# Graph-network kernel on one core: the node half of the gate weight loaded as 32x32 blocks and turned by VectorE

## The chip, the cores and the metric

One Trainium2 chip, one of its cores. The metric is the device time in microseconds of one execution. A core has TensorE (PE, matmul), VectorE (DVE), ScalarE (ACT), GpSimd (POOL) and SyncE (SP), which here only issues transfers; ScalarE can issue transfers too. All engines run their own instruction lists and meet by semaphores. Sixteen DMA engines move data between HBM and SBUF for the core. TensorE contracts over the 128 partitions, so both operands of a product must have the summed index on the partitions; a weight that lies the other way has to be turned first.

## The reference

Eight graphs of eight nodes (64 nodes, 768 features) pass four blocks, each with a residual and a layer norm. The change is in the first block, L0: two rounds of a relational convolution (RGCN) and a gate.

```python
def _gate(h, q, Wg, bg, Wq, bq):
    h3 = h.reshape(B, N, F)
    hg = jnp.einsum('bnf,gf->bng', h3, Wg[:, :F])
    qg = jnp.einsum('blf,gf->blg', q, Wg[:, F:]) + bg
    attn = jax.nn.sigmoid(hg[:, :, None, :] + qg[:, None, :, :])
    qi = jnp.einsum('bnlf,blf->bnf', attn, q)
    alpha = jax.nn.sigmoid(jnp.einsum('bnf,gf->bng', h3, Wq[:, :F]) + jnp.einsum('bnf,gf->bng', qi, Wq[:, F:]) + bq)
    hn = alpha * jnp.tanh(qi) + (1.0 - alpha) * h3
...
h = jax.nn.relu(_rgcn(x, W_rel1, W_root1, b1, src, dst, edge_type))
h = _gate(h, query_embs, Wg, bg, Wq, bq)
h = jax.nn.relu(_rgcn(h, W_rel2, W_root2, b2, src, dst, edge_type))
h = _gate(h, query_embs, Wg, bg, Wq, bq)
```

The gate weight Wg is [768, 1536]. Its left half (the node half) multiplies h, its right half (the query half) the queries. Both are summed over their second index, so both have to be turned. Everything is float32.

## The kernel before

All weights of 768x768 live in seven slots W[0] to W[6] of [128, 6, 768]: row block k of 128 rows is W[s][:, k, :]. The table PLAN says which weight is loaded into which slot and in how many transfers. SyncE issues the weight loads in one written-out order; where a slot is still in use, it waits on a semaphore first, and everything behind it in its list waits too.

TensorE turns a weight in groups: `turn_weight` makes three 128x128 transposes into one PSUM bank (a group), and VectorE or ScalarE copies the bank into the turned weight (`copy_group`). A half of 768x768 takes 12 groups, 36 transposes. Groups are numbered over the whole kernel: the query half of Wg, the queries, the node half (from G_H), and then Wq (from G_QH). The semaphore `turned` counts the groups.

The order of the program up to the first gate is this. TensorE turns the query half and the queries and multiplies them in eight query units (`query_unit`, six chunks each), whose results go to qg. GpSimd meanwhile makes constants and splits the biases into three bfloat16 parts; VectorE builds tables from the edge lists (hot_src in one instruction of 1536 columns, hot_dst in two of 512), from which TensorE counts the edges. Then come the 36 transposes of the node half, which was loaded into slot 3 and goes turned into slot 4 (WgT_h), then the first half of unit 4, the mixing of the nodes (`mix`), the rest of unit 4, and the RGCN: four `project` calls with the three relations and the root weight. Root is loaded into slot 3, so its load waits until the node half is turned. After the RGCN, VectorE takes relu into h, TensorE turns h (with the six EARLY groups of Wq around it) and multiplies it by WgT_h (`project(nodeT, WgT_h, ...)`).

The result hg is split on VectorE into hi, mid and low; ScalarE and GpSimd copy parts of it into `stack`. The first gate then goes over 32 tiles of 128x768. For each tile TensorE spreads rows of the stack (L1395), VectorE adds qg (L913), ScalarE takes the sigmoid (L689), GpSimd (20 tiles, L609) or VectorE (12 tiles, L905) multiplies by the queries, and TensorE sums (L1343). Between the tiles TensorE does the chunks of units 6 and 7 (UNIT_AT) and the other 18 groups of Wq (LATE_AT, from tile 13). Unit 5 (SPLIT_UNIT) stands whole between projection and gate. The second round uses the same turned weights.

At the end of the first gate SyncE loads four small tables into qk (L510, L512), in 768 runs of 16 or 4 bytes each.

## Time and profile before

| | before |
|---|---|
| time, median of 3 runs | 270.37 us (269.51 to 270.51) |
| the profiled execution, its own time | 270.35 us |
| its span (first to last instruction) | 268.5 us |
| granted clock of TensorE | full, in all 40 slices |
| TensorE busy | 251.3 us, 94% |
| VectorE busy | 158.6 us, 59% |
| HBM read | 52.17 MB, 195 GB/s over the span |

Times in the profile are microseconds from the start of the span. TensorE works almost throughout, so its busy share does not tell which of its work matters; the chain of work that ended last does. A busy time of an engine that nobody waits for costs nothing. Instructions that issue transfers are not counted as busy and are shown as SPq or ACTq.

### The profile page before, as it was taken

What the parts mean: (1) busy time and instruction counts of PE and PEld (TensorE: products, weight loads), DVE (VectorE), ACT (ScalarE), POOL (GpSimd) and SP (SyncE); (2) the same over time, 40 slices, a digit from 0 to 9 for tenths busy, and PEclk for the clock granted to TensorE, in tenths of its full rate; (3) what the DMA queues carried; (4) which work ended last, traced back from release to release, by engine and by line L of the source; (5) the groups of instructions that cost most, each with busy time, mean ns of one, the idle gap of its engine ahead of it and who ended that gap; (6) DMA issues with size and microseconds to landing.
All of it is one profiled execution on the core that took longest, in us unless ns stands there. A gap on an engine that the chain in (4) does not pass through costs nothing.

```text
span 268.5 us, 4957 instructions
## 1 busy us (share of the span) xinstructions
PE 251.3 (94%) x2065; PEld 130.9 (49%) x2065; DVE 158.6 (59%) x283; ACT 91.5 (34%) x155; POOL 86.3 (32%) x76
## 2 busy tenths in 40 slices
PE   8899999999999999899999998889998988999994
PEld 4565874454435543356775222224573443435572
DVE  0866450015999999943015999996567267514422
ACT  2323340033657996412001667672302013013000
POOL 7790000003599999700000677870000000000000
PEclk9999999999999999999999999999999999999999
DMA  7999996996002967500699940003999636000001
GB/s 242 373 402 400 402 362 211 379 400 269 2 0 61 410 236 256 102 2 0 163 407 401 402 158 2 0 2 94 363 405 401 264 99 256 0 2 0 2 0 29
DMA packets 21895, 53.46 MB, mean 199 GB/s; under 512 B 4201, under 2 KB 4969, under 8 KB 21874
## 3 DMA queue, kind: packets, MB, share of 16 engines
q1 hardware_dynamic: 21184, 52.82, 53.6%
q10 hardware_dynamic: 690, 0.34, 0.5%
q8 instruction: 16, 0.26, 0.4%
q14 instruction: 5, 0.04, 0.0%
HBM read 52.17 MB, written 0.20 MB: 195 GB/s over the span
## 4 chain that ended last, share of the span: by engine, by line
PE 57%; POOL 17%; DVE 13%; issue 6%; ACT 4%; DMA 2%; SPq 0%; POOLq 0%; DVEq 0%; ACTq 0%
POOL prod L609 13%; PE ps L1137 12%; PE ps L1105 10%; PE ps L1253 6%; POOL W L609 4%; PE ps L1152 4%; PE ps L1079 3%; PE ps L1525 3%; PE ps L1605 3%; PE ps L1222 3%; DMA qn<-in_L_gnn_query_embs 2%; ACT pre L689 2%; DVE prod L905 2%; DVE pre L913 2%; PE ps L1343 2%
## 5 line engine op out<-in xcount | busy, mean ns | idle before, releaser
L609 POOL TENSOR_TENSOR prod<-pre,qn 128x768 f32<-128x768 f32 x28 | 56.0, 2023 | 11.5 <-ACT pre L689 11.5
L913 DVE TENSOR_TENSOR pre<-ps,qg 128x768 f32<-128x768 f32 x46 | 42.9, 950 | 2.0 <-PE ps L1329 0.9
L689 ACT ACTIVATE pre<-pre 128x768 f32<-128x768 f32 x46 | 38.7, 847 | 11.9 <-DVE pre L913 11.1
L1253 PE MATMUL ps<-W 128*128 128x384 f32 x96 | 34.7, 490 | 0.8 <-DVE W L457 0.5
L457 ACT COPY W<-ps 128x384 f32<-128x384 f32 x41 | 18.4, 483 | 39.4 <-PE ps L1079 39.2
L689 ACT ACTIVATE ps<-ps 128x768 f32<-128x768 f32 x18 | 14.2, 794 | 29.6 <-PE ps L1329 21.4
L1343 PE MATMUL ps<-prod,rsel 128*32 128x384 f32 x192 | 20.5, 496 | 3.4 <-POOL prod L609 2.7
L1253 PEld LDWEIGHTS ps<-W 128*128 128x128 f32 x96 | 17.3, 190 | 10.7 <-issue 2.0
L1137 PE MATMUL ps<-W,prod 128*64 128x256 f32 (+1 forms) x240 | 20.6, 328 | 0.0
L1079 PE MATMUL ps<-ident,W 128*128 128x128 f32 x144 | 19.7, 278 | 0.6 <-DMA W<-in_L_gnn_Wg 0.6
L1079 PEld LDWEIGHTS ps<-ident,W 128*128 128x128 f32 x144 | 16.9, 143 | 4.1 <-issue 1.3
L905 DVE TENSOR_TENSOR prod<-pre,qn 128x768 f32<-128x768 f32 x12 | 17.7, 1485 | 0.0
L1137 PEld LDWEIGHTS ps<-W,prod 128*64 128x64 f32 x240 | 15.1, 137 | 4.9 <-issue 0.5
L1222 PE MATMUL ps<-bsel 96*128 96x512 bf16 x62 | 16.9, 381 | 0.0
L1395 PE MATMUL ps<-stack,bsel 96*128 96x384 bf16 x64 | 15.8, 329 | 0.3 <-DVE pre L913 0.3
L1105 PE MATMUL ps<-W,prod 128*64 128x384 f32 x96 | 15.6, 486 | 0.0
L595 POOL COPY stack<-hi 32x384 bf16<-32x384 bf16 x2 | 1.2, 611 | 44.5 <-DVE hi L872 44.4
L457 DVE COPY W<-ps 128x384 f32<-128x384 f32 x15 | 8.3, 556 | 11.3 <-PE ps L1079 10.6
L1105 PE MATMUL ps<-W,nodeT 128*64 128x384 f32 x72 | 12.8, 492 | 0.0
L1137 PE MATMUL ps<-W,nodeT 128*64 128x256 f32 (+1 forms) x144 | 12.7, 328 | 0.0
L975 DVE CUSTOM_DVE_ANT_0 qn<-W,pre 128x768 bf16<-128x768 f32 x12 | 11.5, 955 | 1.7 <-DVE prod L975 1.7
L609 POOL TENSOR_TENSOR W<-pre,qn 128x768 f32<-128x768 f32 x6 | 10.9, 1824 | 3.2 <-ACT pre L689 3.2
(242 smaller groups left out, 333.8 us busy)
## 6 DMA issues: line engine op xcount, KB each, us to landing
W<-in_L_gnn_W SPq DMA_DIRECT2D x9, 2304.0 KB, 11.8
W<-in_L_gnn_W_rel SPq DMA_DIRECT2D x6, 2304.0 KB, 15.8
W<-in_L_gnn_W_root SPq DMA_DIRECT2D x2, 2304.0 KB, 9.5
W<-in_L_gnn_Wq SPq DMA_DIRECT2D x4, 1152.0 KB, 7.9
W<-in_L_gnn_Wg SPq DMA_DIRECT2D x3, 1152.0 KB, 13.2
qn<-in_L_gnn_query_embs SPq DMA_DIRECT2D x4, 384.0 KB, 10.2
W<-in_L_gnn_Wg SPq DMA_DIRECT2D x3, 384.0 KB, 3.9
W<-qg SPq DMA_DIRECT2D x2, 384.0 KB, 4.9
```

What stands on the lines that cost most here:

```text
L457: ins = nc.vector.tensor_copy(dst, src) if done is turned_out_v else nc.scalar.copy(dst, src)
L609: nc.gpsimd.tensor_tensor(prod_of(T), pre_of(T), qn[:, pair_and_node(t)[0], :], ALU.mult).then_inc(prod_p, 1)
L689: nc.scalar.activation(tile, tile, ACT.Sigmoid).then_inc(sig_ready, 1)
L905: nc.vector.tensor_tensor(by_half(prod_of(T)), src, by_half(qn[:, pair_and_node(T % TILES)[0], :]), ALU.mult).then_inc(prod_v, 1)
L913: nc.vector.tensor_tensor(dst, ring(T), by_half(qg[:, pair_and_node(T % TILES)[0], :]), ALU.add).then_inc(pre_ready, 1)
L1079: ins = nc.tensor.transpose(ps[:, group_bank(g), at:at + P], src, ident[:, :])
L1105: ins = nc.tensor.matmul(ps[c * N:(c + 1) * N, bank, 0:HD], T[:, j, col0 + h * N:col0 + (h + 1) * N], w[:, k, c * HD:(c + 1) * HD], start= ...
L1137: ins = nc.tensor.matmul(wide(bank)[c * N:(c + 1) * N, cols], T[:, j, col0 + h * N:col0 + (h + 1) * N], w[:, k, c * HD + cols.start:c * HD ...
L1222: nc.tensor.matmul(ps[:, bank, :], bsel[0:3 * GN, 0, :], bsel[0:3 * GN, 0:4, :].rearrange("p a b -> p (a b)"), start=True, stop=True, skip ...
L1253: ins = nc.tensor.matmul(ps[:, unit_bank(u), 0:HD], qT[:, k, p * P:(p + 1) * P], WgT_q[:, k, c * HD:(c + 1) * HD], start=(k == 0), stop=(k ...
L1343: ins = nc.tensor.matmul(ps[at:at + GN, ACC, 0:HD], rsel[:, s:s + GN], prod_of(T + g)[:, c * HD:(c + 1) * HD], start=first, stop=last, ski ...
L1395: ins = nc.tensor.matmul(ring(t)[:, c, :], bsel[0:3 * GN, t // 2, :], stack[:, c, t % 2, :], start=True, stop=True)
```

## The change

The node half of Wg is no longer loaded in whole rows and turned by TensorE. `load_blocks` makes 24 transfers of 96 KB: for each of the six column chunks k and each quarter q of 32 partitions, it puts 24 blocks of 32x32 side by side, so that each run in HBM is 32 elements, 128 bytes. Twelve of them (q = 0, 2) are issued by SyncE behind the last relation, twelve (q = 1, 3) by ScalarE behind its mixing copies. Each chunk lands directly in slot 4, and VectorE turns its 32x32 blocks in place, one instruction for a chunk, before it takes relu(h). The chunks come in the order BY_BLOCK, in which the projection uses them, and the projection waits for each.

Since slot 3 is free, root is loaded ahead of the last relation and without a wait. The EARLY groups of Wq move behind the projection; unit 5 is cut up (two chunks and one around the turning of h, one behind the projection, two at tile 1); units 6 and 7 start two tiles later; ScalarE copies the early groups between its copies into the stack. GpSimd starts to split the biases only when all three edge tables are there.

```diff
-    PLAN = [("Wg_q", 0, 2), ("Wg_h", 3, 2), ("rel1_0", 5, 1), ...
+    PLAN = [("Wg_q", 0, 2), ("Wg_h", 4, 6), ("rel1_0", 5, 1), ...
...
-        G_QH = G_H + GROUPS
+        G_QH = G_H
...
-        EARLY = (0, 1, 2, 5, 6, 7)
+        EARLY = (0, 1, 2, 3, 6, 7)
...
-        UNIT_AT = {t: (SPLIT_UNIT + 1 + i, k) for i in range(2) for k in range(KC) for t in [i * (KC + 1) + k]}
+        UNIT_AT = {t: (SPLIT_UNIT + 1 + i, k) for i in range(2) for k in range(KC) for t in [2 + i * (KC + 1) + k]}
...
+        def load_blocks(eng, first):
+
+            for k in BY_BLOCK:
+                for q in range(first, P // GN, 2):
+                    f = k * P + q * GN
+                    eng.dma_start(WgT_h[q * GN:(q + 1) * GN, k, :].rearrange("p (b i) -> p b i", i=GN),
+                                  a["L0_gnn_Wg"][:, f:f + GN].rearrange("(b p) i -> p b i", p=GN)).then_inc(loaded["Wg_h"][k], 16)
...
-            load("Wg_h", Wg[:, 0:D])
             load("rel1_0", a["L0_gnn_W_rel1"][0])
             load("rel1_1", a["L0_gnn_W_rel1"][1])
+            load("root1", a["L0_gnn_W_root1"])
             load("rel1_2", a["L0_gnn_W_rel1"][2], turned, G_Q1)
-            load("root1", a["L0_gnn_W_root1"], turned, G_QH)
+            load_blocks(sp, 0)
...
             link(nc.gpsimd.memset(biases[:, :], 0.0))
+            pool.wait_ge(hot_ready, 3)
             pool.wait_ge(bias_loaded, 16 * nb)
...
                 mix_copy(layer)
                 if layer == 0:
-                    for k in range(len(EARLY)):
-                        copy_group(act, G_QH + k, turned_out_s)
+                    load_blocks(act, 1)
...
-                if layer == 0:
-                    unit_copy(SPLIT_UNIT)
-                    act.wait_ge(qg_out_s, act_units(SPLIT_UNIT + 1))
+                    for k in range(0, 2) if i == 0 else range(2, len(EARLY)):
+                        copy_group(act, G_QH + k, turned_out_s)
...
                     unit_copy(SPLIT_UNIT - 1)
+                    for k in BY_BLOCK:
+                        dve.wait_ge(loaded["Wg_h"][k], 16 * (P // GN))
+                        nc.vector.transpose(WgT_h[:, k, :], WgT_h[:, k, :]).then_inc(WgT_h_ready, 1)
...
-            for k in range(GROUPS):
-                turn_weight(G_H, "Wg_h", k)
...
                     wait_units_out(pe, SPLIT_UNIT)
-                    turn_wq(range(0, 3))
+                    query_unit(SPLIT_UNIT, range(0, 2))
                     turn_nodes(hh, ident, node_turned, NODE_BANKS[:1], made=(h_ready, 1))
-                    turn_wq(range(3, len(EARLY)))
+                    query_unit(SPLIT_UNIT, range(2, 3))
                     add_bias("L0_gnn_bg", HG0)
-                    project(nodeT, WgT_h, HG0, first=False, waits=as_copied(nodeT_ready, 1)).then_inc(hg_done, 1)
-                    wait_groups_out(pe, G_QH + len(EARLY))
-                    query_unit(SPLIT_UNIT)
+                    pe.wait_ge(nodeT_ready, 2)
+                    project(nodeT, WgT_h, HG0, first=False,
+                            waits={i: (WgT_h_ready, i + 1) for i in range(KC)}).then_inc(hg_done, 1)
+                    turn_wq(range(0, len(EARLY)))
+                    query_unit(SPLIT_UNIT, range(JC, JC + 1))
+                    wait_groups_out(pe, G_QH + JC + 1)
```

On TensorE, from the turning of the last queries (qn) to the start of the gate, the program reads so before. L1079 are transposes, W3 the node half as loaded, W5 the first part of Wq; L1253 are query units, L1105 the products of the RGCN and, with nodeT, the gate projection.

```order
L1079 MATMUL ps<-ident,qn 128x128 x12
L1079 MATMUL ps<-ident,W3 128x128 x36
L1253 MATMUL ps<-W1,W2 128x384 x3
L1269 MATMUL ps<-adjT,xa 128x256 x6
L1253 MATMUL ps<-W1,W2 128x384 x3
...
L1079 MATMUL ps<-ident,W5 128x128 x9
L1206 MATMUL ps<-ident,hh 128x128 x3
L1079 MATMUL ps<-ident,W5 128x128 x9
L1123 MATMUL ps<-biases,i4 64x384 x2
L1105 MATMUL ps<-W4,nodeT 64x384 x12
L1253 MATMUL ps<-W1,W2 128x384 x6
```

The same stretch of the changed kernel, where L1090, L1262, L1114 and L1215 are the same lines moved down:

```order
L1090 MATMUL ps<-ident,qn 128x128 x12
L1262 MATMUL ps<-W1,W2 128x384 x3
L1278 MATMUL ps<-adjT,xa 128x256 x6
L1262 MATMUL ps<-W1,W2 128x384 x3
...
L1262 MATMUL ps<-W1,W2 128x384 x2
L1215 MATMUL ps<-ident,hh 128x128 x3
L1262 MATMUL ps<-W1,W2 128x384
L1132 MATMUL ps<-biases,i4 64x384 x2
L1114 MATMUL ps<-W4,nodeT 64x384 x12
L1090 MATMUL ps<-ident,W5 128x128 x18
L1262 MATMUL ps<-W1,W2 128x384
```

The 36 transposes are gone, the 18 of Wq stand behind the projection, and unit 5 is spread around them.

On SyncE, the loads behind the queries stand so before (W3, W5, W6 and W0 are the slots):

```order
L478 DMA W3<-in_L0_gnn_Wg 128x3x768 x2
L478 DMA W5<-in_L0_gnn_W_rel1 128x6x768
L478 DMA W6<-in_L0_gnn_W_rel1 128x6x768
L478 DMA W0<-in_L0_gnn_W_rel1 128x6x768
L478 DMA W3<-in_L0_gnn_W_root1 128x6x768
L478 DMA W5<-in_L0_gnn_Wq 128x3x768 x2
```

and so in the changed kernel:

```order
L486 DMA W5<-in_L0_gnn_W_rel1 128x6x768
L486 DMA W6<-in_L0_gnn_W_rel1 128x6x768
L486 DMA W3<-in_L0_gnn_W_root1 128x6x768
L486 DMA W0<-in_L0_gnn_W_rel1 128x6x768
L471 DMA W4<-in_L0_gnn_Wg 32x24x32 x12
L486 DMA W5<-in_L0_gnn_Wq 128x3x768 x2
```

The node half is last of the six weights now, in small runs, and Wq stands behind it. On ScalarE the other twelve stand between the mixing copies and the first copy into the stack:

```order
L650 COPY qg<-ps 128x384
L664 COPY prod<-ps 128x4x64 x3
L471 DMA W4<-in_L0_gnn_Wg 32x24x32 x12
L676 COPY stack<-hi 32x384 x2
L457 COPY W0<-ps 128x384 x2
L676 COPY stack<-mid 32x384 x2
```

Before, six group copies into W0 stood in the place of the transfers, and none between the copies into the stack.

## Rows read from the trace of the kernel before

**Rows 1.** The page, busy us, share of the span and instructions of each engine.

```profile
PE 251.3 (94%) x2065; PEld 130.9 (49%) x2065; DVE 158.6 (59%) x283; ACT 91.5 (34%) x155; POOL 86.3 (32%) x76
```

**Rows 2.** The chain that ended last, 12 to 70 us: start, length, engine and line.

```profile
16.75 2.17 PE ps L1253 x6
...
30.38 5.24 PE ps L1079 x48
...
37.56 1.50 PE ps L1269 x12
...
41.47 15.48 PE ps L1105 x96
56.95 1.13 PE ps L1079 x9
...
58.41 0.98 PE ps L1079 x9
...
59.68 3.90 PE ps L1105 x24
...
63.60 0.57 DVE hi L872
...
68.08 0.97 DVE pre L913
```

**Rows 3.** Timeline of TensorE: start, busy us, instructions.

```profile
31.53 4.09 PE L1079 MATMUL ps<-ident,W 128*128 128x128 f32 x36
...
63.48 4.14 PE L1253 MATMUL ps<-W 128*128 128x384 f32 x12
```

**Rows 4.** Timelines of VectorE and GpSimd, 10 to 16 us.

```profile
10.63 1.76 DVE L771 TENSOR_TENSOR prod<-pre 128x1536 bf16<-128x1536 f32 x1
12.31 3.36 DVE L775 TENSOR_TENSOR prod<-pre 128x512 bf16<-128x512 f32 x2
...
11.94 1.13 POOL L581 CAST biases<-bias 9x768 bf16<-9x768 f32 x1 [1.57 <-DMA bias<-in_L_gnn_b]
13.15 1.97 POOL L582 TENSOR_TENSOR bias<-bias,biases 9x768 f32<-9x768 f32 x1
```

**Rows 5.** Timelines of ScalarE and GpSimd, 38 to 113 us.

```profile
38.26 1.24 ACT L656 COPY prod<-ps 128x256 f32<-128x256 f32 x3 [2.46 <-PE ps L1269]
57.47 2.55 ACT L457 COPY W<-ps 128x384 f32<-128x384 f32 x6 [17.97 <-PE ps L1079]
64.19 1.04 ACT L669 COPY stack<-hi 32x384 bf16<-32x384 bf16 x2 [4.17 <-DVE hi L872]
...
70.12 16.47 POOL L609 TENSOR_TENSOR prod<-pre,qn 128x768 f32<-128x768 f32 x8 [3.07 <-ACT pre L689]
87.13 8.05 POOL L609 TENSOR_TENSOR prod<-pre,qn 128x768 f32<-128x768 f32 x4 [0.54 <-ACT pre L689]
95.48 16.86 POOL L609 TENSOR_TENSOR prod<-pre,qn 128x768 f32<-128x768 f32 x8 [0.30 <-ACT pre L689]
```

**Rows 6.** Busy time by window, in the gate; last three: clock, DMA share, GB/s.

```profile
85.00:90.00 5.00, 5.00 (x43) 2.87 (x41) 4.70 (x5) 4.93 (x11) 4.46 (x3) 1.00 0.89 306
```

**Rows 7.** The same view of five other windows (columns PE, PEld, DVE, ACT, POOL).

```profile
34.00:36.00 2.00, 2.00 (x17) 1.84 (x16) 1.71 (x4) 1.44 (x3) 0.00 (x0) 1.00 1.04 404
36.50:37.00 0.50, 0.50 (x3) 0.31 (x2) 0.00 (x0) 0.00 (x0) 0.00 (x0) 1.00 1.14 369
...
46.00:46.50 0.50, 0.50 (x6) 0.17 (x4) 0.00 (x0) 0.00 (x0) 0.00 (x0) 1.00 0.48 49
...
109.25:112.25 3.00, 3.00 (x30) 1.13 (x30) 2.95 (x4) 2.30 (x3) 3.00 (x2) 1.00 0.47 16
110.50:111.50 1.00, 1.00 (x12) 0.27 (x12) 0.95 (x2) 0.95 (x2) 1.00 (x2) 1.00 0.10 2
```

**Rows 8.** Issues: a start on SyncE's timeline; the output's line with KB and landing.

```profile
45.38 4.77 SPq L478 DMA_DIRECT2D W<-in_L_gnn_Wq  x4
...
out<-t SPq DMA_DIRECT2D x1, 96.0 KB, 2.2
```

More of the change, by code:

```diff
@@ L35, in gnn_kernel @@
     assert N == 64 and 2 * L == P and 2 * HD == D and KC % 2 == 0
-    PLAN = [("Wg_q", 0, 2), ("Wg_h", 3, 2), ("rel1_0", 5, 1), ("rel1_1", 6, 1), ("rel1_2", 0, 1), ("root1", 3, 1),
+    PLAN = [("Wg_q", 0, 2), ("Wg_h", 4, 6), ("rel1_0", 5, 1), ("rel1_1", 6, 1), ("rel1_2", 0, 1), ("root1", 3, 1),
             ("Wq_h", 5, 2), ("Wq_q", 6, 2), ("rel2_0", 3, 1), ("rel2_1", 2, 1), ("rel2_2", 5, 1), ("root2", 6, 1),
@@ L175, in gnn_kernel @@
         loaded = {key: [sem(f"{key}_{c}_loaded") for c in range(n)] for key, _, n in PLAN}
+        WgT_h_ready = sem("WgT_h_ready")
         Wg_q_rows = [sem(f"Wg_q_rows_{i}") for i in range(JC)]
@@ L409, in unit_on_act @@
             return u % 2 == 1 or u >= SPLIT_UNIT
+        BY_BLOCK = [h * JC + j for j in range(JC) for h in range(2)]
         MIX_BANKS = (((1, 5), (2, 6), (3, 7)), ((0, 3), (1, 4), (2, 5)))
@@ L443, in group_dst @@
                 return qT[:, i * JC:(i + 1) * JC, p * P:(p + 1) * P]
-            if g < G_QH:
-                k = g - G_H
-                return WgT_h[:, k % KC, (k // KC) * HD:(k // KC + 1) * HD]
             k = (g - G_QH) % GROUPS
@@ L650, in _ @@
             unit_copy(3)
-            copy_groups(G_H, G_QH)
             def mix_copy(layer):
@@ L670, in _ @@
                                        part[h * N:h * N + GN, :]).then_inc(stacked[0], 1)
-                if layer == 0:
-                    unit_copy(SPLIT_UNIT)
-                    act.wait_ge(qg_out_s, act_units(SPLIT_UNIT + 1))
+                    for k in range(0, 2) if i == 0 else range(2, len(EARLY)):
+                        copy_group(act, G_QH + k, turned_out_s)
                 for t in range(TILES):
                     T = layer * TILES + t
+                    if (layer, t) == (0, 2):
+                        unit_copy(SPLIT_UNIT)
                     if layer == 0:
@@ L1094, in turn_weight @@
                 turn_blocks(g0 + k, [src[:, part * JC + i, col * P:(col + 1) * P] for i in range(JC)])
-            BY_BLOCK = [h * JC + j for j in range(JC) for h in range(2)]
             def project(T, w, bank, first=True, last=True, col0=0, chunks=BY_BLOCK, waits={}):
@@ L1299, in _ @@
                 turn_queries(G_Q1 + 2 * (i - 1), PAIRS[i])
-            for k in range(GROUPS):
-                turn_weight(G_H, "Wg_h", k)
             pe.wait_ge(x_loaded, 32)
             pe.wait_ge(adj_ready, 2)
+            wait_groups_out(pe, G_Q1 + 4)
+            query_unit(4, HALF1)
             wait_units_out(pe, 4)
-            query_unit(4, HALF1)
             wait_groups_out(pe, G_QH)
@@ L1397, in first_gate @@
                         ins.then_inc(hg_cast, 1)
+                        if t == 1:
+                            query_unit(SPLIT_UNIT, range(JC + 1, KC))
+                            wait_groups_out(pe, G_QH + len(EARLY))
                         if t in UNIT_AT:
```

## The prediction

> **What bounds the kernel now.** I read the busy table first. TensorE is busy 94% of the span, VectorE 59%, and no other engine is near it [rows 1]. That share alone says little, so I followed the chain that ended last. From 16.75 to 63.6 us it runs almost only through TensorE: query units, 48 transposes that end at 35.6, the node mixing at 37.56, the four RGCN products at 41.47 for 15.48 us, the turning of h, the gate projection at 59.68 [rows 2]. From 63.6 it goes through VectorE (the split of the projection in three parts, 4.48 us to the first add at 68.08), and from 70.12 through GpSimd, which multiplies with 0.84 us of idle time (0.54 and 0.30) until 112.3 [rows 2, 5]. So each microsecond by which the first add comes earlier ends the first gate a microsecond earlier, and all that follows waits for that gate. What matters is the path to 68.08.
>
> **The 36 transposes go.** The node half costs TensorE one row of 36 transposes at 31.53, 4.09 us, and on the chain nothing hides it: the query unit behind it starts at its end, 35.62 [rows 2, 3]. Now that unit follows the 12 transposes of the queries. They end at 31.53, and the unit also waits for VectorE's copy of one of their groups, for which I allow 0.1 us. It starts at 31.65 in place of 35.46, so mixing and RGCN come 3.8 us earlier. The data of the RGCN is no obstacle: the queue carries as many bytes ahead of the last relation as before (root in place of the node half). The queue runs at 404 GB/s up to 36 and falls off near 36.8 (369 from 36.5 to 37) [rows 7]: all four weights are there before the third product begins. **-3.8 us.**
>
> **The bias split moves behind the edge tables.** The first table, 1536 columns, took 1.76 us; the two of 512 columns took 3.36 us together, 1.68 each, though each has a third of the work. Exactly over these two GpSimd ran its cast and its subtraction (11.94 to 15.1) [rows 4]. At the first table's rate they cost 0.6 each, so the tables would be ready 2.1 us earlier. Of this only what TensorE waited counts: it had finished the unit before by about 16.2 and began the next at 16.75, after VectorE's copies behind the tables [rows 2]. So 0.5 us of the 2.1 reaches the path. The bounds are 0 (the tables are slow by themselves) and 0.6. GpSimd's split then lasts from about 13.6 to 21.5, and TensorE reads it at 37: 15 us of cover. **-0.5 us.** (The Trainium skill, page "SBUF — State Buffer", section "SBUF: two separate sides", says that a VectorE operation with two SBUF inputs and a GpSimd operation exclude each other for a whole instruction. The rows agree; the sum would be the same.)
>
> With both, the RGCN runs from 37.2 to 52.6, in place of 41.47 to 56.95.
>
> **Between RGCN and projection.** Before: nine transposes (1.13), the turning (0.33), nine transposes (0.98), the bias: 2.73 us to the projection at 59.68 [rows 2]. Now: two chunks of query unit 5, the turning, one chunk, the bias. A unit of six chunks took 4.14, a chunk 0.69 [rows 3], so 1.3 + 0.33 + 0.65 + 0.3 = 2.6. **0 us.** The projection begins at 55.3 and the cast to hi at 59.2, if the weight is there.
>
> **Start of the gate.** Behind the projection TensorE now has 18 transposes (2.0 us) and one chunk. That leaves it free at 62.0, and VectorE's stack is done at 63.7 (59.2 + 4.48), so both are hidden. ScalarE is not: it copies hi (1.04), two groups (0.43 each), mid (1.04) and two groups more, in that order, and the first tile needs four groups out of its banks [rows 5]. Mid is ready near 60.8, so: hi to 60.8, groups to 61.7, mid to 62.7, groups to 63.6; then the matmul, 0.35. The first add starts at 64.1 to 64.2, 0.45 later than its own inputs allow. **+0.45 us.** Bounds 0 and 1.
>
> **Inside the gate.** The units move by two tiles, so tiles 13 and 14 hold a chunk and late transposes at once, 1.3 us more on TensorE than before, where it was already full (5.00 of 5 us from 85 to 90); tile 1 holds two chunks. GpSimd had 0.54 us of idle time in that stretch [rows 6]. With four buffers ahead of GpSimd most is absorbed. **+0.3 us**, bounds 0 and 1.3.
>
> **The loads in 128-byte runs.** This is what decides. 24 transfers of 768 runs are 18,432 runs, 1,152 for each of 16 DMA engines. SP's half is queued behind the last relation and starts near 36.8. ScalarE's half is issued when the third mixing copy is dispatched, at 39.1 before, now 34.8; a transfer issued at 45.38 showed its first traffic in the window from 46 [rows 5, 7, 8], so it starts between 35.7 and 36.8. No row shows 128-byte runs from HBM. Nearest are the four small loads at the end of the gate, 3,072 runs of 4 to 16 bytes, 192 for each engine. In the 3.00 us from 109.25, when the large load ahead of them was through, the DMA engines were busy for 0.47 of the time, 1.41 us: 7.3 ns a run. By the clock, idle stretches included, it is 3.00 us: 15.6 ns [rows 7]. The bytes themselves cost 128 B at 25 B/ns (404 GB/s over 16) = 5.1 ns. If the bytes hide behind the fixed part, a run costs 7.3 ns and all take 8.4 us; if they add, 12.4 ns and 14.3 us; at worst 15.6 + 5.1 = 20.7 ns and 23.8 us. I take 11 ns, nearer to the sum, since no row here shows bytes that hide: 12.7 us, so the last run is at 49.5. Landing costs about 1.1 (a 96 KB output took 2.2 us from issue, of which 0.85 is start and 0.25 bytes) [rows 8].
>
> VectorE turns each chunk as it lands. No row has its transpose; an add of the same 128x768 took 0.97 us [rows 2], and I take that, with 2x as upper bound. Five of six turns lie beside the loads; the last ends at 49.5 + 1.1 + 1.0 = 51.6, and VectorE needs to be free at 52.6. **0 us, with 1.0 us of margin.** If the cover is gone, VectorE stands in its queue before relu(h), and behind that stand node turning, projection, the split and the whole gate: one microsecond late is one microsecond on the end.
>
> (The Trainium skill, page "DMA: Bandwidth & Descriptors", section "Why small descriptors are slow (HBM only)", gives three extra cycles of 32 bytes per packet. For 128 bytes that is 7 cycles for 4, an estimate of 230 GB/s at this kernel's 404, so 10.3 us for the 2.36 MB; the sum would not change.)
>
> **Sum.** -3.8 - 0.5 + 0 + 0.45 + 0.3 + 0 = -3.55. The profiled run took 270.35 us, the median is 270.37, so they can be used alike: **266.8 us**.
>
> **The rivals.** (1) *The runs are slow, and VectorE waits.* From 36.8 the loads may take until 52.6 - 2.1 = 50.5, 11.9 ns a run; at 15.0 ns the delay is 3.55 us and the change gives nothing; beyond that it is slower. At 20.7 ns the last run starts at 60.6, relu at 62.7, and the time is 276.9. For it: the clock price of 15.6 ns for runs a tenth the size, and reads that hop over rows 6 KB apart. Against: those loads met idle stretches, with a share of 0.10 from 110.5 to 111.5 [rows 7], so the clock is not their rate. A delay over 3.55 us gets 0.14. (The same page of the Trainium skill, section "Specifications", says that below 512 bytes a transfer becomes a read-modify-write. If it doubled the 11 ns taken here, this rival's 20.7 ns and its 276.9 would hold; the small loads were below 512 bytes too and cost 7.3 ns with it, so the rule stays inside this rival's 0.14.)
>
> (2) *One queue trails the other.* As soon as SP's half is through, the Wq loads follow in 3 KB runs, each 3072/25 = 0.12 us, and if the engines serve the two queues in turn, each remaining run of ScalarE's queue waits for one. Thirty trailing runs cost 3.7 us, of which the margin takes 1.0: 269.5. This needs ScalarE's queue to start 0.3 us after SP's; the start times above make them even. 0.14, near no change.
>
> (3) *The gate gives it back.* TensorE at tiles 13 and 14 costs the whole 1.3 us and ScalarE's copies 1: 266.8 + 1.6 = 268.4. TensorE's small idle time speaks for it, GpSimd's buffers against. 0.12, still faster.
>
> (4) *The bias part does nothing*: 267.3, inside the first case.
>
> **How the numbers follow.** Forecast 0.60, rivals 0.14, 0.14, 0.12. 0.5% is 1.35 us, about what a measurement of this kernel can tell from no change. Faster by more than that (below 269.0): 0.60 + 0.12 + 0.03 of rival 2, whose lag may be shorter, 0.75. Slower (above 271.7): 0.11 of rival 1 and 0.02 of rival 2, 0.13. The same: what is left, 0.12. The likeliest case spans 265.9 (gate terms zero) to 268; the range reaches to 271.2 to take in rival 2, rival 3 and the start of rival 1.
>
> **What would show it.** Right: the mixing at about 33.2 and RGCN from 37.2 to 52.6 without a gap; the two 512-column tables at about 0.6 us each; six transposes on VectorE, the last before 52.6; the first add near 64.1, GpSimd's first multiply near 66.2. Wrong: a wait of VectorE on a DMA ahead of its last transpose or ahead of relu; DMA windows from 37 on below 150 GB/s; ScalarE's half landing clearly after SP's, with large traffic beside it.

## The result, and the profile after

The changed kernel takes 268.94 us (median of 20 runs, 267.54 to 276.15), the kernel before 270.32 (20 runs, 269.51 to 270.55): a ratio of 0.9941, 95% interval 0.9925 to 0.9957. That is faster, but by 1.4 us where 3.55 were forecast. The runs scatter much more than before: seven of the 20 lie between 267.54 and 267.70, the others above. The ratio is one of means and leaves out as slow the four longest runs, 271.88 to 276.15. They are also the ones with the lowest mean granted clock of TensorE, 0.985 to 0.992, where all others have 0.996 to 1.000; a longer wait of TensorE would do both (experiments 2 and 4), but none of the four has a profile. The profiled execution took 268.83 us, with a span of 267.0.

The busy table of the changed kernel, where 36 matmuls are gone [rows 1]:

```profile
PE 248.0 (93%) x2029; PEld 127.5 (48%) x2029; DVE 158.7 (59%) x283; ACT 88.4 (33%) x149; POOL 84.2 (32%) x76
```

The chain of the changed kernel that ended last, 33 to 66 us:

```profile
33.52 1.55 PE ps L1278 x12
...
37.15 3.39 ACTq L471
...
47.38 6.43 DMA W<-in_L_gnn_Wg
53.83 0.98 DVE W L860
54.81 0.19 DVE hh L865
...
56.74 3.90 PE ps L1114 x24
60.66 0.57 DVE hi L883
...
65.68 0.97 DVE pre L924
```

Where [rows 2] had only TensorE from 16.75 up to the projection, the chain now passes through ScalarE's issues (ACTq L471), the transfer of the last chunk and its transpose. The timelines of TensorE (before, then changed) and of VectorE show both sides of that meeting:

```profile
41.30 15.65 PE L1105 MATMUL ps<-W,prod 128*64 128x384 f32 x96
```

```profile
37.26 15.65 PE L1114 MATMUL ps<-W,prod 128*64 128x384 f32 x96
```

```profile
12.32 1.28 DVE L783 TENSOR_TENSOR prod<-pre 128x512 bf16<-128x512 f32 x2
...
49.61 0.98 DVE L860 STREAM_TRANSPOSE W<-W 128x768 f32<-128x768 f32 x1 [0.87 <-DMA W<-in_L_gnn_Wg]
53.83 0.98 DVE L860 STREAM_TRANSPOSE W<-W 128x768 f32<-128x768 f32 x1 [3.24 <-DMA W<-in_L_gnn_Wg]
54.73 0.58 DVE L865 TENSOR_SCALAR hh<-ps 128x128 f32<-128x128 f32 x2
```

The RGCN ends at 52.91 (before: 56.95), but VectorE still waits for a chunk, and relu comes only at 54.73. The two tables of [rows 4] take 1.28 us together in place of 3.36.

The account, as shifts of the changed kernel against the one before, between the same points of both: RGCN start 41.30 to 37.26 on the timelines, -4.04; from the RGCN's end to the projection 2.73 to 3.83 (52.91 to 56.74), +1.10; from hi to the first add 4.48 to 5.02, +0.54; from there to the first multiply 2.04 to 1.99, -0.05; GpSimd's 20 multiplies, first start to last end, 42.22 to 43.16, +0.94. The sum is -1.51, and the span is 1.5 shorter. GpSimd's timeline in the changed kernel has the idle time of the gate:

```profile
67.67 16.46 POOL L618 TENSOR_TENSOR prod<-pre,qn 128x768 f32<-128x768 f32 x8 [3.54 <-ACT pre L697]
84.93 1.83 POOL L618 TENSOR_TENSOR prod<-pre,qn 128x768 f32<-128x768 f32 x1 [0.81 <-ACT pre L697]
87.07 1.83 POOL L618 TENSOR_TENSOR prod<-pre,qn 128x768 f32<-128x768 f32 x1 [0.31 <-ACT pre L697]
90.06 3.62 POOL L618 TENSOR_TENSOR prod<-pre,qn 128x768 f32<-128x768 f32 x2 [1.16 <-ACT pre L697]
94.21 16.62 POOL L618 TENSOR_TENSOR prod<-pre,qn 128x768 f32<-128x768 f32 x8 [0.54 <-ACT pre L697]
```

It is idle for 2.82 us in four pieces, where it was idle for 0.84 in two [rows 5]; its 20 multiplies take 40.36 us in place of 41.38, so that 0.94 of the 1.98 remain. Why they are shorter isn't shown.

### The profile page after: what moved, and what is told of

Read it like the earlier page. It is cut to its first block, busy times and chain, and to the rows that moved or that the text cites. A ratio compares the mean times of both kernels' runs of the same rounds, so it can differ in the third digit from the quotient of the medians.

```text
span 267.0 us, 4901 instructions
## 1 busy us (share of the span) xinstructions
PE 248.0 (93%) x2029; PEld 127.5 (48%) x2029; DVE 158.7 (59%) x283; ACT 88.4 (33%) x149; POOL 84.2 (32%) x76
## 4 chain that ended last, share of the span: by engine, by line
PE 52%; POOL 14%; DVE 9%; ACT 7%; DMA 6%; issue 6%; ACTq 4%; SPq 1%; DVEq 0%; POOLq 0%
PE ps L1146 12%; POOL prod L618 10%; PE ps L1262 7%; DMA W<-in_L_gnn_Wg 6%; ACTq L471 4%; POOL W L618 4%; PE ps L1114 4%; PE ps L1161 4%; PE ps L1539 3%; PE ps L1619 3%; ACT pre L697 3%; PE ps L1231 3%; PE ps L1351 2%; PE ps L1090 2%; DVE prod L916 2%
## 5 line engine op out<-in xcount | busy, mean ns | idle before, releaser
L618 POOL TENSOR_TENSOR prod<-pre,qn 128x768 f32<-128x768 f32 x28 | 54.9, 1981 | 14.0 <-ACT pre L697 13.9
L1262 PE MATMUL ps<-W 128*128 128x384 f32 x96 | 35.0, 490 | 0.4 <-ACT W L457 0.4
L457 ACT COPY W<-ps 128x384 f32<-128x384 f32 x35 | 15.6, 484 | 21.0 <-PE ps L1090 20.9
L1262 PEld LDWEIGHTS ps<-W 128*128 128x128 f32 x96 | 17.2, 190 | 9.6 <-issue 1.3
L1090 PE MATMUL ps<-ident,W 128*128 128x128 f32 x108 | 16.0, 287 | 0.9 <-DMA W<-in_L_gnn_Wg 0.7
L1090 PEld LDWEIGHTS ps<-ident,W 128*128 128x128 f32 x108 | 13.4, 148 | 5.0 <-issue 1.4
L1114 PE MATMUL ps<-W,prod 128*64 128x384 f32 x96 | 15.7, 486 | 0.0
L1114 PE MATMUL ps<-W,nodeT 128*64 128x384 f32 x72 | 12.8, 492 | 0.0
L860 DVE STREAM_TRANSPOSE W<-W 128x768 f32<-128x768 f32 x6 | 5.9, 978 | 11.2 <-DMA W<-in_L_gnn_Wg 11.1
```

What stands on the lines that cost most here:

```text
L457: ins = nc.vector.tensor_copy(dst, src) if done is turned_out_v else nc.scalar.copy(dst, src)
L618: nc.gpsimd.tensor_tensor(prod_of(T), pre_of(T), qn[:, pair_and_node(t)[0], :], ALU.mult).then_inc(prod_p, 1)
L1090: ins = nc.tensor.transpose(ps[:, group_bank(g), at:at + P], src, ident[:, :])
L1114: ins = nc.tensor.matmul(ps[c * N:(c + 1) * N, bank, 0:HD], T[:, j, col0 + h * N:col0 + (h + 1) * N], w[:, k, c * HD:(c + 1) * HD], start= ...
L1262: ins = nc.tensor.matmul(ps[:, unit_bank(u), 0:HD], qT[:, k, p * P:(p + 1) * P], WgT_q[:, k, c * HD:(c + 1) * HD], start=(k == 0), stop=(k ...
```

## The experiments

Each ratio is to the kernel before, with its 95% interval. All edits are to the changed kernel, but for the one that says otherwise.

**1. Does Wq's load delay ScalarE's half?** SyncE, whose own half is issued first, waits until all chunks have landed before it issues Wq (`wq_waits`):

```diff
             load_blocks(sp, 0)
+            for k in range(KC):
+                sp.wait_ge(loaded["Wg_h"][k], 16 * (P // GN))
             load("Wq_h", Wq[:, 0:D], rgcn_done, 1)
```

> SyncE waits until all six chunks of the node half are there before it issues the loads of Wq. Theory T (trailing): what made VectorE wait in the profiled execution is ScalarE's last 128-byte runs taking turns with the 3 KB runs of Wq. Then the last chunk is there before 53.0 us, VectorE does not wait ahead of relu, all executions lie within about 0.3 us of each other and the time is 267.6 us, the lowest that the changed kernel showed. Theory R (rate): the runs themselves are slow by a random amount. Then the last chunk still lands at 53 to 54 in some executions and the spread of 267.5 to 276 stays, median near 269.

Measured: 267.78 us (267.74 to 267.85), 0.9912 (0.9899 to 0.9926). VectorE's timeline of this kernel:

```profile
51.55 0.98 DVE L862 STREAM_TRANSPOSE W<-W 128x768 f32<-128x768 f32 x1 [0.85 <-DMA W<-in_L_gnn_Wg]
52.92 0.62 DVE L867 TENSOR_SCALAR hh<-ps 128x128 f32<-128x128 f32 x2 [0.38 <-PE ps L1116]
```

The last chunk is there 2.3 us earlier, and VectorE now waits for the RGCN and not for a chunk. TensorE's chain of this kernel has nothing but its work between the two products:

```profile
52.86 1.49 PE ps L1264 x4
...
55.61 3.90 PE ps L1116 x24
```

This also tells what a late relu costs. In the changed kernel it came 1.81 us later than here (54.73 against 52.92), but 3.83 - 2.75 = 1.08 us of that reached the projection: the two chunks of unit 5, 1.49 us of TensorE's work ahead of the turning, covered the rest. The scatter is gone too, here and in the nine runs of experiment 5 (266.51 to 268.12 over two kernels, 0.4 us at most within one), so I put it down to this meeting, which can fall differently from run to run; only one run of the changed kernel has a profile. How the two queues meet is seen in the changed kernel's DMA queues (packets, MB, share), first from 49 to 50 us, then from 51 to 52:

```profile
q10 hardware_dynamic: 1058, 0.13, 85.2%
q1 hardware_dynamic: 126, 0.04, 23.2%
```

```profile
q1 hardware_dynamic: 117, 0.36, 99.2%
q10 hardware_dynamic: 12, 0.00, 0.9%
```

q10 is ScalarE's queue. From 51 a dozen stragglers share the DMA engines with Wq, whose 3 KB runs take 99% of their time; from 52 to 54 seven more of ScalarE's runs appear, and the chunk counts as landed with the last. Each queue had 9,216 short runs to move. SyncE's began at 36.9 and ScalarE's at 38.3, but by 40 ScalarE's had nearly caught up (253 runs behind). Then its fourth issue, which lasts from 37.15 to 40.54 in the chain above, left it with little to move: it was 1,104 behind at 42 and 1,100 at 49. In experiment 1 it trailed as well, by 667 at 49, and both were through by 51.2: trailing without Wq did no harm.

**2. The same loss made large, and the check on it.** ScalarE issues its half only when the first product of the RGCN is done, at 41 (`scalar_late`), and that once more with experiment 1's wait of SyncE (`scalar_late_wq_waits`):

```diff
                 if layer == 0:
+                    act.wait_ge(rgcn_done, 1)
                     load_blocks(act, 1)
```

> The changed kernel, with ScalarE's twelve transfers held back until the first relation's product is done (about 41.2 us). Theory T (taking turns with Wq): SyncE's half is through near 45, then 96 runs of 3 KB of Wq on each engine follow at once, and ScalarE's remaining runs take turns with them for 12 us: the last chunk lands at 57 to 63, VectorE waits, and the time is 273 to 284. Rival (the runs only queue by bytes): Wq does not matter, the last chunk lands near 52, and the time is 268 to 269.

> The same hold on ScalarE's half, but Wq's loads wait for all chunks. Theory T: the last chunk lands at 51 to 52.5 and the time is 267.8 to 268.4, so the whole loss of scalar_late is Wq's company. Rival: the late start by itself makes the loss, and the time is that of scalar_late.

Measured: 288.81 us (288.45 to 289.60), 1.0692 (1.0674 to 1.071), and with SyncE waiting 268.61 (268.35 to 269.50), 0.9946 (0.993 to 0.9963). DMA queues of the first from 54 to 62 us, VectorE's timeline, and windows of TensorE (last columns clock, DMA share, GB/s):

```profile
q1 hardware_dynamic: 1006, 2.94, 95.5%
q10 hardware_dynamic: 1003, 0.13, 10.1%
```

```profile
64.87 0.98 DVE L861 STREAM_TRANSPOSE W<-W 128x768 f32<-128x768 f32 x1 [14.56 <-DMA W<-in_L_gnn_Wg]
69.84 1.84 DVE L861 STREAM_TRANSPOSE W<-W 128x768 f32<-128x768 f32 x2 [3.99 <-DMA W<-in_L_gnn_Wg]
```

```profile
52.00:54.00 2.00, 2.00 (x8) 0.68 (x4) 0.00 (x0) 0.00 (x0) 0.00 (x0) 1.00 1.04 397
...
56.00:58.00 2.00, 0.00 (x0) 0.00 (x0) 0.00 (x0) 0.00 (x0) 0.00 (x0) 0.87 1.05 380
58.00:60.00 2.00, 0.00 (x0) 0.00 (x0) 0.00 (x0) 0.00 (x0) 0.00 (x0) 0.50 1.06 388
```

1,006 packets of one queue beside 1,003 of the other: the DMA engines serve the queues in turn, one run each, whatever the runs' size. In short windows too the counts are nearly even (59 and 59 from 56 to 56.5, when an engine passes four of each), so turns of many runs are excluded. A 128-byte run so waits for a 3 KB one each time, 0.13 us, and 125 of ScalarE's runs pass in a microsecond, where 825 pass beside SyncE's short ones (4,127 from 42 to 47 in the changed kernel). TensorE idles from 54, and its granted clock has fallen to 0.50, 1.2 GHz, by 58 and makes the rest slower as well. The second kernel, with the same late issue, loses 0.8 us to experiment 1 and not 21: nearly all of the loss is Wq's company, not the late issue. Both numbers lie beyond what theory T gave (273 to 284, and 267.8 to 268.4): the last chunk landed at 69.8 and not at 57 to 63, with the clock on top, and in the second kernel the last transpose ended at 54.2, 1.7 us later than in experiment 1. (The Trainium skill, page "DMA: Bandwidth & Descriptors", section "Queues, rings and completion order", has the DMA engines take turns by packets of some 9 to 17 descriptors. The runs here agree with the turns, but not with that size: one run against one.)

**3. Are the short runs themselves a cost?** The node half as six loads of whole 3 KB rows from SyncE alone, VectorE's transposes as they are. This leaves out the placing of the blocks that the product needs (`rows_3kb`):

```diff
-            load_blocks(sp, 0)
+            for k in BY_BLOCK:
+                sp.dma_start(WgT_h[:, k, :], Wg[k * P:(k + 1) * P, 0:D]).then_inc(loaded["Wg_h"][k], 16)
...
-                if layer == 0:
-                    load_blocks(act, 1)
...
-                        dve.wait_ge(loaded["Wg_h"][k], 16 * (P // GN))
+                        dve.wait_ge(loaded["Wg_h"][k], 16)
```

> The node half is loaded in whole 3 KB rows by SyncE at the same place, and VectorE turns 32x32 blocks of it in place: this leaves out the right placing of the blocks, so the output is not the reference's; it shows what the short runs cost. Theory T: 2.36 MB in 5.9 us end at 43, nothing waits, 267.6 us, the same as with short runs whose landing is in time. Theory R would also give 267.6 here; if the time is clearly below 267.3, the short runs cost something else than the wait of VectorE.

Measured: 267.73 us (267.66 to 267.76), 0.991 (0.9896 to 0.9923). VectorE's timeline:

```profile
40.12 5.85 DVE L858 STREAM_TRANSPOSE W<-W 128x768 f32<-128x768 f32 x6 [2.42 <-DMA W<-in_L_gnn_Wg]
52.92 0.62 DVE L863 TENSOR_SCALAR hh<-ps 128x128 f32<-128x128 f32 x2 [6.95 <-PE ps L1112]
```

The weight is turned by 45.97, 6.6 us earlier than in experiment 1, and the time is the same within 0.1 us: short runs cost nothing once they arrive ahead of relu.

**4. What does the second issuing queue give?** All 24 transfers on SyncE (`one_queue`, `load_blocks(sp, 0, step=1)` and none on ScalarE); then 12 of twice the size, which leave out the right source of each block (`one_queue_pairs`), and 48 of half the size (`one_queue_halves`). The first edit below is that of `one_queue`, the second comes on top of it for the 48; that for the 12 isn't shown, and there two chunks share a transfer, so VectorE turns them in pairs.

```diff
-                for q in range(first, P // GN, 2):
+                for q in range(first, P // GN, step):
...
-            load_blocks(sp, 0)
+            load_blocks(sp, 0, 1)
...
-                if layer == 0:
-                    load_blocks(act, 1)
```

```diff
-                    eng.dma_start(WgT_h[q * GN:(q + 1) * GN, k, :].rearrange("p (b i) -> p b i", i=GN),
-                                  a["L0_gnn_Wg"][:, f:f + GN].rearrange("(b p) i -> p b i", p=GN)).then_inc(loaded["Wg_h"][k], 16)
+                    for h in range(2):
+                        eng.dma_start(WgT_h[q * GN:(q + 1) * GN, k, h * HD:(h + 1) * HD].rearrange("p (b i) -> p b i", i=GN),
+                                      a["L0_gnn_Wg"][h * HD:(h + 1) * HD, f:f + GN].rearrange("(b p) i -> p b i", p=GN)).then_inc(loaded["Wg_h"][k], 16)
```

> All 24 transfers issued by SyncE, none by ScalarE, Wq behind them in the same queue. Theory T: one queue cannot trail itself; the engines work at 10.5 ns a run in either case, so the last chunk lands near 51, no spread, 267.6 us. Rival: one queue alone does not keep the engines busy (13 ns a run or the issue of 24 transfers at 0.5 us each limits it); then the last run is at 36.8 + 15 = 51.8 or later, the chunk lands at 53 or later and the time is 268.5 to 269.5.

> One queue once more, but 12 transfers of 192 KB (1,536 runs of 128 bytes each) in place of 24 of 96 KB. The access pattern of such a transfer has no room for the right source, so the values loaded are others: the output isn't the reference's; bytes, runs and run length are the same. Theory I (with 24 transfers SyncE's issuing was the bound: 0.53 us each with 0.04 between them, and the DMA engines ran dry): with half as many issues the loads end when two queues end them, so the last transpose begins at 51 to 52, relu doesn't wait, and the time is 267.8 (ratio 0.991). Rival Q (the DMA engines take 14 ns a run from one queue and 10.5 from two): nothing changes, the last transpose begins near 55 and the time is 272.6 (ratio 1.009).

> One queue, but 48 transfers of 48 KB (384 runs each). Theory I, with an issue that costs 0.53 us whatever it moves: about 44 of the issues follow each other from 39.6 at 0.57 each, the last one at 64.7, the last transpose near 67, and the time is near 285 (ratio 1.055), TensorE's clock included. Theory I', with an issue that costs by the run (0.27 us each), and rival Q: the same 55 and 272.6 as with 24.

Measured: 272.62 us (271.67 to 273.39), 1.0089 (1.0067 to 1.0111); with 12 transfers 272.07 (271.45 to 272.32), 1.0078 (1.0059 to 1.0096); with 48 281.31 (280.53 to 282.76), 1.0423 (1.0387 to 1.0458). For the first, theory T's 267.6 fell: the rate of one queue is another than that of two. Its rival named this but gave too low a time (268.5 to 269.5). With 12 transfers rival Q's 272.6 held. With 48 theory I held in kind, with 281.3 in place of 285: an issue took 0.47 us and not 0.53. Windows of DMA (clock, DMA share, GB/s) of the changed kernel, then of the one with a single queue:

```profile
42.00:44.00 2.00, 1.00 1.26 196
44.00:46.00 2.00, 1.00 1.23 192
46.00:48.00 2.00, 1.00 1.28 199
```

```profile
42.00:44.00 2.00, 1.00 0.98 157
44.00:46.00 2.00, 1.00 0.95 146
46.00:48.00 2.00, 1.00 0.88 138
```

One queue moves 147 GB/s there, two 196. The one-queue chain shows SyncE's issues back to back, most at 0.53 us, so the issuing looked like the bound. Half as many issues, though, leave relu at 55.79 in place of 55.89. They did help at the start: some 1,100 more runs were through from 38 to 42, and the last landing came at 54.01 in place of 54.97, which the two transposes behind it took back. But from 42 to 47 the rate is the same (5,822 runs against 5,856), and the issues themselves stretch (median 1.43 us, shortest 0.78), as if they waited for room in the queue: theory I fell for 24. So a single queue runs at about 14 ns a run and DMA engine (128 B at 147/16 GB/s), two together at 10.5. With 48 transfers the issues do bind. Rows of that kernel's chain:

```profile
53.76 0.47 SPq L472
...
60.93 3.14 DMA W<-in_L_gnn_Wg
```

An issue costs 0.47 us for 384 runs, 0.53 for 768 and at most 0.78 (the shortest) for 1,536: mostly by the transfer, less by the run. (The Trainium skill, the same page, section "Issuing engines are not separate DMA queues", says that several issuing engines only save issue time. For 128-byte runs they also gave a third more rate here.) The DMA queues from 42 to 47 us, first of the one-queue kernel, then of the changed one, tell where it comes from:

```profile
q1 hardware_dynamic: 5856, 0.74, 95.0%
```

```profile
q10 hardware_dynamic: 4127, 0.52, 66.5%
q1 hardware_dynamic: 3613, 0.45, 59.0%
```

A packet takes 13 ns in all three (its queue's share of 16 engines times 5 us, by its packets). One queue's packets follow each other on an engine every 13.7 ns, nearly back to back; with two queues one comes every 10.3 ns and the shares add up to 125%, so packets of the two overlap. What lets them isn't shown.

In the one-queue kernel TensorE is idle for 1.95 us ahead of the turning of h, and the projection after it takes longer, in windows of TensorE:

```profile
56.00:58.00 2.00, 1.80 (x7) 0.85 (x9) 1.03 (x3) 0.00 (x0) 0.00 (x0) 0.83 0.99 375
58.00:60.00 2.00, 2.00 (x10) 0.72 (x8) 0.00 (x0) 0.00 (x0) 0.00 (x0) 0.50 1.03 415
60.00:62.00 2.00, 2.00 (x14) 0.85 (x12) 0.00 (x0) 0.00 (x0) 0.00 (x0) 0.82 1.02 413
```

VectorE waits 5.83 us for the projection in place of 4.19, and 1.3 of these 1.6 us are the projection's own (5.19 in place of 3.90): the delay is paid a second time in the clock. In the changed kernel the idle time was 0.64 and the clock stayed at 1.00.

**5. What costs 0.9 us inside the gate?** On top of experiment 1, ScalarE copies a finished unit ahead of the late groups of the tile (`wq_waits_copy`), or units and late groups no longer meet: unit 7's chunks on tiles 8 to 13, the late groups on tiles 14 to 25 (`wq_waits_tiles`):

```diff
+                    if layer == 0 and UNIT_AT.get(t, (0, 0))[1] == KC - 1:
+                        unit_copy(UNIT_AT[t][0])
                     if layer == 0:
...
-                    if layer == 0 and UNIT_AT.get(t, (0, 0))[1] == KC - 1:
-                        unit_copy(UNIT_AT[t][0])
```

```diff
-        LATE_AT = sorted([13 + 2 * k for k in range(LATE - GROUPS)] + [TILES - KC - GROUPS - 1 + k for k in range(GROUPS)])
+        LATE_AT = sorted([14 + 2 * k for k in range(LATE - GROUPS)] + [TILES - KC - GROUPS + k for k in range(GROUPS)])
-        UNIT_AT = {t: (SPLIT_UNIT + 1 + i, k) for i in range(2) for k in range(KC) for t in [2 + i * (KC + 1) + k]}
+        UNIT_AT = {t: (SPLIT_UNIT + 1 + i, k) for i in range(2) for k in range(KC) for t in [2 + i * KC + k]}
```

> As wq_waits, and ScalarE copies a finished query unit before the group copies of the same tile, not after them. In the profile of the changed kernel VectorE waited 1.22 us at 87 for ScalarE's copy of unit 7, and GpSimd's gate was 0.94 us longer than before. Theory C (copy order): this wait goes, the gate takes 42.3 us from GpSimd's first to last multiply as before in place of 43.2, and the time is 0.8 to 0.95 us below wq_waits: 266.7. Rival P (TensorE): the gate is longer because TensorE has a chunk and late transposes in tiles 13 and 14; then the time stays within 0.2 us of wq_waits.

> As wq_waits (267.78 us), with unit 7's chunks in tiles 8 to 13 in place of 9 to 14, and the late groups of Wq one tile later (14 to 25 in place of 13 to 24), so that no tile holds a chunk and late transposes. The copy order of ScalarE was not the cause (267.79). Theory P (TensorE): with no idle time from 79.7 to 88 it is what makes VectorE wait 1.21 us at tile 16; then this wait goes, the gate takes 42.2 to 42.4 us from GpSimd's first to last multiply and the time is 0.7 to 0.95 us less, 266.9 to 267.1. Rival: the gate is longer for another reason (the two chunks at tile 1, the moved banks), and the time stays at 267.8.

Measured: 267.79 us (267.71 to 268.12), 0.9916 (0.9902 to 0.993), for the first; 266.61 (266.51 to 266.66), 0.9866 (0.9851 to 0.9881), for the second. VectorE's wait in the gate, without the early copy and with it:

```profile
87.16 0.96 DVE L926 TENSOR_TENSOR pre<-ps,qg 128x768 f32<-128x768 f32 x1 [1.21 <-ACT qg L652]
```

```profile
87.19 0.96 DVE L926 TENSOR_TENSOR pre<-ps,qg 128x768 f32<-128x768 f32 x1 [1.21 <-PE ps L1405]
```

The same 1.21 us under another name: ScalarE's copy was only the last of two things that came together, and theory C fell. With the tiles moved the wait is gone, and GpSimd's timeline reads

```profile
66.36 20.75 POOL L620 TENSOR_TENSOR prod<-pre,qn 128x768 f32<-128x768 f32 x10 [3.54 <-ACT pre L699]
87.82 3.63 POOL L620 TENSOR_TENSOR prod<-pre,qn 128x768 f32<-128x768 f32 x2 [0.71 <-ACT pre L699]
...
100.33 8.27 POOL L620 TENSOR_TENSOR prod<-pre,qn 128x768 f32<-128x768 f32 x4 [0.30 <-ACT pre L699]
```

From 66.36 to 108.60 is 42.24 us, as before the change (42.22). The whole +0.94 was the meeting of chunks and late transposes on tiles 13 and 14. The time fell by 1.17 us and not by 0.7 to 0.95: 0.16 of it is TensorE's earlier begin in the profiled run (12.11 in place of 12.27). Two things aren't shown: which of the two moves is needed, and that a full TensorE is the reason. It was busy 5.00 of 5 us from 82.5 to 87.5 in the changed kernel, but also there before the change and from 88 to 93 with the tiles moved, without the loss.

**6. The start of the gate.** TensorE waits for two early groups ahead of tile 0 and for four ahead of tile 1 (`wq_waits_start`, on top of experiment 1):

```diff
-                    wait_groups_out(pe, G_QH + JC + 1)
+                    wait_groups_out(pe, G_QH + 2)
...
+                    if t == 1:
+                        wait_groups_out(pe, G_QH + JC + 1)
                     if t < 2:
```

> Beside the Wq loads that wait for the node half, TensorE waits for only two of ScalarE's early group copies ahead of tile 0 and for all four ahead of tile 1. Theory S (the first tile waits for ScalarE's copies of the third and fourth group, behind mid): the first add starts about 0.5 us earlier against the end of the projection, TensorE's wait for a group copy ahead of L1403 goes, and the time is 267.3, 0.5 below the kernel whose only edit is the waiting Wq. Rival (the gate is filled by TensorE at tiles 8 to 14 and not by its start): the first add comes 0.5 earlier and the time stays at 267.8, with that much more idle time of GpSimd inside the gate.

Measured: 267.18 us (266.94 to 267.43), 0.9891 (0.9878 to 0.9905). From hi to the first add it takes 4.48 us (59.30 to 63.78) in place of 5.02, as before the change, and the gate's 43.20 stays: 0.54 us are gained and kept.

**7. The bias split.** GpSimd's wait for the tables taken out of experiment 1's kernel (`wq_waits_bias`), and put alone into the kernel before the change (`bias_alone`):

```diff
             link(nc.gpsimd.memset(biases[:, :], 0.0))
+            pool.wait_ge(hot_ready, 3)
```

> As wq_waits (267.78 us), without GpSimd's wait for the edge tables (that part of the change undone). The two 512-column tables took 0.64 us each in the changed kernel and 1.68 before. Theory B (port shared with GpSimd): they take 1.68 again, TensorE starts its second query unit 0.55 us later, and the time is 268.3. Rival: TensorE's own path hides it, and the time stays at 267.8.

> The kernel before, with GpSimd's wait for the three edge tables ahead of the bias split as its only edit. Theory B (the tables are slowed by GpSimd's instructions beside them): the two 512-column tables take 1.3 us together in place of 3.4, the RGCN starts 0.5 us earlier, and the time is 269.8 with a smaller spread than that of the kernel before, which falls on about 269.6 and 270.35. Rival (the tables are slow for another reason, or something else than they is waited for): 270.3 and two values as before.

Measured: without the wait 268.28 us (four runs from 268.26 to 268.31, one of 267.54), 0.9923 (0.991 to 0.9935); alone 269.64 (269.47 to 270.07, 11 runs), 0.9984 (0.9975 to 0.9993). In the second VectorE's two tables take 1.29 us, and TensorE's chain has the RGCN at 40.72, 0.75 before [rows 2]:

```profile
12.30 1.29 DVE L776 TENSOR_TENSOR prod<-pre 128x512 bf16<-128x512 f32 x2
```

```profile
40.72 15.48 PE ps L1106 x96
```

Of the 0.75 us, 0.55 are the tables'; the other 0.2 come from the first weight's load, with which TensorE began at 12.11 here and at 12.32 in the changed kernel. So the wait is worth 0.3 to 0.7 us (by ratios 0.3 and 0.4, by medians 0.5 and 0.7). The profiled run without it is the one of 267.54, and there GpSimd's cast begins at 12.60 and not at 11.94, since its own load came later, and the tables take 1.91 together: how far the two overlap hangs on that load. The smaller spread that I expected of the wait alone did not show.

**8. All of it** (`all_fixes`): experiments 1, 5 (both edits) and 6 together.

> The waiting Wq loads, the chunks of unit 7 at tiles 8 to 13 with the late groups at 14 to 25, ScalarE's unit copy ahead of its group copies, and the start of the gate with two groups. If the 1.2 us of the tiles and the 0.5 us of the start add, 266.1 (ratio 0.984); if the start is swallowed by the gate, 266.6, as with the tiles alone.

Measured: 266.32 us (266.29 to 266.70), 0.9864 (0.9849 to 0.9879), the fastest version. In its profile the start gives its 0.54 (hi at 59.63, first multiply at 66.10) and the gate takes 42.20. Against the tiles alone (0.9866) the ratios are the same within their intervals, so the times don't settle whether the start's 0.5 us add to the whole (266.1 was forecast). In the profiles they do: this run is 0.3 us shorter than that of the tiles alone though TensorE began 0.26 us later (12.37 and not 12.11), on the first weight's load. Noise of that size hides what is left to find.

## Why the prediction was right or wrong

The mechanisms were all named, but the forecast put two that were listed as rivals at nothing or nearly so, and so came out 2.0 us too low in the profiled run (1.10 + 0.64 + 0.3 + 0.1 for loads, gate, transposes and start of the gate).

- **Transposes, -3.8**: -3.49 measured (4.04 less 0.55). Right in kind, 0.3 us too much: the unit waited 0.20 us for ScalarE's copy of the last group and not 0.1, and the mixing came at 33.5 and not at 33.2.
- **Bias split, -0.5**: TensorE began its last transposes at 29.83 in place of 30.38 [rows 2], -0.55, and experiment 7 shows it both ways, with its profile for the wait alone. Right.
- **Between RGCN and projection, 0**: the work alone takes 2.75 us in experiment 1 (52.86 to 55.61), before 2.73. Right.
- **Start of the gate, +0.45**: 0.54, by the mechanism given; experiment 6 takes it back. Right.
- **Inside the gate, +0.3**: 0.94. Here the step failed in its size: "With four buffers ahead of GpSimd most is absorbed." Most was not: of the 1.3 us of extra work on tiles 13 and 14 the gate paid 0.94, and all of it went when chunks and late transposes no longer met (experiment 5). This is the mechanism of rival 3. That TensorE had been full in that stretch already [rows 6] fits, but isn't shown to be the reason.
- **The loads, "0 us, with 1.0 us of margin"**: +1.10 us in the profiled run. This is the step that failed most, and what failed in it is that the two queues were taken to run even because their start times were ("the start times above make them even"). ScalarE's queue started at 38.3 and not "between 35.7 and 36.8", 1.4 us behind SyncE's, had made up most of that by 40 and then fell 1,100 runs behind, as experiment 1 tells; so its half was still under way when Wq's 3 KB runs came. That is rival 2, which had a chance of 0.14. At 49 SyncE had at most 126 short runs left and ScalarE 1,244 (1,058 to 50, 186 after), 70 more for each DMA engine, and the 12 for each that were left beside Wq after 50 were enough. The rival's 30 trailing runs were too many and its 269.5 a little high.
- **The price of a run, 11 ns**: 10.5 with both queues under way, but the whole took longer. In experiment 1 all runs were through at 51.2 and not at 49.5, 12.5 ns for each from 36.8 on, with a dip from 40 to 41 (662 runs, where 1,430 passed in the microsecond before) and one queue alone at the end. The last chunk had landed 0.35 us later in place of 1.1, so the last transpose ended at 52.53 and not at 51.6, and 0.38 us of margin to relu were left in place of 1.0. Without Wq the loads are in time all the same.
- **"One microsecond late is one microsecond on the end"**: too strict. Relu 1.81 us late cost 1.08, since TensorE still had two chunks of unit 5 to do, which the prediction itself had put there.
- **Rival 1** (slow runs) fell: 128-byte runs from HBM cost 10.5 ns, far from 20.7. Its condition was near, though: with one queue, at 14 ns, the change makes the kernel slower (experiment 4), where the rival had put the limit at 15.0.

With the loads and the tiles mended the time is 266.6, and with the start of the gate as well 266.3: the forecast of 266.8 is near what the change gives once Wq waits and the tiles don't meet. That is partly luck: the transposes gave 0.3 us less than forecast and the gate then cost 0.3 less.

## What to carry to other kernels

When the last transfers that somebody waits for go over two queues, look at what each queue holds behind them: the first queue to finish brings its next load, and large runs in it hold up the other's small ones run by run. One wait on the landing of both, ahead of the next load, gave 0.8 us (by the ratios; 1.2 by the medians) and an even time here, and cost at most 0.3 us against the changed kernel's own best runs (267.74 to 267.85 against 267.54 to 267.70). Two lots of extra work on the same tile cost 0.94 us that they did not cost a tile apart, and a wait that is taken away can merely change its name (experiment 5), so test the engine behind it before mending what the profile names.

## What the hardware showed unexpectedly

- The DMA engines serve two queues run by run: 1,006 packets of 3 KB against 1,003 of 128 bytes in 8 us.
- 128-byte runs from HBM: 196 GB/s over two issuing queues, 147 over one, also with transfers of twice the size from 42 us on. A packet takes 13 ns either way; those of two queues overlap.
- An issue costs SyncE 0.47, 0.53 and at most 0.78 us for 384, 768 and 1,536 runs.
- VectorE turns the 32x32 blocks of 128x768 float32 in 0.98 us, as long as an add (0.97).
- A table of 512 columns on VectorE took 0.64 us alone and 1.68 beside GpSimd's instructions; the one of 1,536 columns, 1.76 in both kernels, with GpSimd idle in the changed one and for all but the last 0.4 us of it before.
- An idle stretch of 2 us on TensorE was followed by a granted clock of 0.50 and 1.3 us more for the next projection; one of 0.64 us by neither.
